# MLP layer of a two-layer kernel: part of the first activation and the add of x on GpSimd, the feature read from its PSUM bank, four more second-layer blocks on VectorE

## The reference

```python
f = lrelu(conv1x1(gn(x), sw1, sb1))      # 128 -> 64
f = lrelu(conv1x1(f, sw2, sb2))          # 64 -> 32
f = conv1x1(f, sw3, sb3)                 # 32 -> 16
# feat: the 16 features of each pixel, joined with one of 128 depth points in -1..1
h = lrelu(conv1x1(feat, mw1, mb1))       # 17 -> 32, for each point
h = lrelu(conv1x1(h, mw2, mb2))          # 32 -> 32
h = lrelu(conv1x1(h, mw3, mb3))          # 32 -> 16
x = x + sigmoid(conv1x1(h, mw4, mb4))    # 16 -> 1, the points are the channels
```

## Time and profile before

| | us |
|---|---|
| median of 3 runs | 9821.51 (9809.74 to 9825.37) |
| profiled execution | 9827.07 |
| its span, first to last instruction | 9825.2 |

### The profile page before, as it was taken

One profiled execution on the slowest core, in us unless ns is written; L12 is line 12 of the kernel. 1 busy time (PEld: TensorE's weight loads), 2 busy tenths in 40 slices (PEclk: granted clock), 3 DMA queues, 4 the chain that ended last, 5 costly groups with the idle time before them and its releaser, 6 DMA issues. The chain is left out here.

```text
span 9825.2 us, 453859 instructions
## 1 busy us (share of the span) xinstructions
PE 9314.5 (95%) x201050; PEld 3949.9 (40%) x201050; DVE 8993.4 (92%) x10311; ACT 8370.6 (85%) x14741; POOL 5791.9 (59%) x2564
## 2 busy tenths in 40 slices
PE   7999998999899999899989999989998999998999
PEld 4555553222455555222245555522224555552222
DVE  6999998999699999899979999989997999998998
ACT  5888887999778888799978788879997887887999
POOL 5999993000699999300069999930007999992000
PEclk9999998999999999899999999999999999999999
DMA  3333331000233333100023333310002333321000
GB/s 102 81 82 88 83 84 44 31 31 27 66 81 87 84 81 86 40 31 31 27 69 87 81 81 84 84 43 29 30 27 73 87 81 82 87 80 32 21 22 18
DMA packets 377226, 605.60 MB, mean 62 GB/s; under 512 B 96962, under 2 KB 98148, under 8 KB 374756
## 3 DMA queue, kind: packets, MB, share of 16 engines
q1 hardware_dynamic: 370752, 574.99, 21.0%
q10 hardware_dynamic: 4516, 1.57, 0.1%
HBM read 236.45 MB, written 71.30 MB: 31 GB/s over the span
## 5 line engine op out<-in xcount | busy, mean ns | idle before, releaser
L927 DVE TENSOR_TENSOR_SCAN arena<-arena,carried,ps 128x512 f32<-128x512 f32 x3968 | 4754.3, 1261 | 294.2 <-PE ps L446 287.9
L815 POOL TENSOR_TENSOR arena<-arena 128x1024 f32<-128x1024 f32 x2048 | 4798.2, 2382 | 148.1 <-PE ps L457 53.2
L975 DVE SCALAR_TENSOR_TENSOR arena<-arena,neg_p 128x512 f32<-128x512 f32 x4096 | 2762.8, 747 | 0.4
L699 ACT ACTIVATE arena<-arena,a_neg 128x512 f32<-128x512 f32 x4096 | 2662.8, 710 | 35.6 <-DVE arena L927 30.8
L446 PE MATMUL ps<-arena 64*32 64x128 f32 x131072 | 2335.8, 275 | 107.9 <-DVE arena L927 57.5
L754 ACT ACTIVATE arena<-ps,b2t 128x512 f32<-128x512 f32 x3840 | 2334.8, 699 | 70.3 <-PE ps L540 44.3
L446 PEld LDWEIGHTS ps<-arena 64*32 64x32 f32 x131072 | 1849.8, 106 | 1234.4 <-DVE arena L927 696.5
L823 POOL TENSOR_TENSOR arena<-arena 128x1024 f32<-128x1024 f32 x128 | 307.6, 2403 | 2969.7 <-DVE arena L919 2968.2
L540 PE MATMUL ps<-arena,w2s 32*32 32x512 f32 x32768 | 1578.5, 603 | 53.6 <-ACT arena L754 35.5
L761 ACT ACTIVATE arena<-ps,bm 128x1024 f32<-128x1024 f32 x1024 | 1165.3, 1138 | 6.1 <-PE ps L551 6.1
L551 PE MATMUL ps<-arena,m 64*32 64x512 f32 x16384 | 1120.7, 599 | 8.6 <-ACT arena L761 4.9
(11 more groups left out here) (111 smaller groups left out, 6570.0 us busy)
## 6 DMA issues: line engine op xcount, KB each, us to landing
arena<-arena SPq DMA_DIRECT2D x4096, 64.0 KB, 2.0
arena<-c_d SPq DMA_DIRECT2D x1024, 128.0 KB, 2.9
xr<-in_x SPq DMA_DIRECT2D x128, 256.0 KB, 3.2
x_d<-xr SPq DMA_DIRECT2D x128, 256.0 KB, 3.3
xr<-x_d SPq DMA_DIRECT2D x128, 256.0 KB, 3.0
out<-arena SPq DMA_DIRECT2D x128, 256.0 KB, 2.0
xs<-in_x SPq DMA_DIRECT2D x96, 256.0 KB, 3.2
arena<-in_x SPq DMA_DIRECT2D x4, 2048.0 KB, 14.9
```

Source lines behind the costliest of these rows:

```text
L699: A(dA[(UNITS * t + m) % DR][:, gi, :], drep[:, e, :], ACT.Exp, scale=a_neg[:, e, 2 * gp + gi:2 * gp + gi + 1]).then_inc(s_dA, 1)
L815: nc.gpsimd.tensor_tensor(hc[m % CR], H[:, m % HR, :, :], crep[:, 2 * gp:2 * gp + 2, :], ALU.mult).then_inc(s_ch, 1)
L927: V.tensor_tensor_scan(H[:, m % HR, gi, :], dA[(UNITS * t + m) % DR][:, gi, :], dbu[m % 2].rearrange("p (l g) -> p g l", g=2)[:, gi, :], 0 ...
L975: m = V.scalar_tensor_tensor(out=t1[k % 4][:, q, :], in0=g[par], scalar=neg_p[:, i:i + 1], in1=gs_[par], op0=ALU.max, op1=ALU.add)
```

## The change

1. SHARED goes from (1, 3) to (0, 1, 2, 3, 4, 6): VectorE does bank 3 of leaky2 in six groups, ScalarE 26 blocks per chunk instead of 30. VectorE's two instructions are rewritten: the first makes 0.01 (m2 + bias) in one pass, the second takes the maximum of (m2 + bias), read from PSUM again, and that. mm2's second half waits for the second one (s_hv) instead of the first (s_hb).
2. BY_POOL: of leaky1's four blocks Pool does block 3 in even groups and blocks 2 and 3 in odd groups, 12 of 32 per chunk. It uses a tensor_scalar (max) for each block, from `g`, and one tensor_tensor (add of `gs_`, repeated over the blocks) for each group. mm2 waits for s_lp too.
3. VectorE's leaky1 reads the feature from `f_ps` in PSUM for all groups (LATE = 8). The bank must hold until the chunk's last leaky1, so the feature's first two products go to bank 6 (`m4_ps`), between one chunk's sigmoid and the next one's first mm4, and the third product waits for s_l1 of all eight groups.
4. The order moves: the feature products go to k = 2, 3 and 5, mm4 to k = 4, 5, 7 (and 1), `spread_g` to k = 6, and leaky2(k) comes before leaky1(k+2) on VectorE.
5. The sdf add goes to Pool, behind its leaky1(4), and for the last chunk of a batch element behind its leaky1(7).

```diff
-SHARED = (1, 3)
+SHARED = (0, 1, 2, 3, 4, 6)
+BY_POOL = ((3,), (2, 3))
+R1, AHEAD, LATE = 4, 2, 8
@@ features, tensor engine
-                    pe.wait_ge(s_g, t)
-                    mm(f_ps[0:64], s1r[:, :], xr[place], start=True, stop=True).then_inc(s_f1, 1)
+                    pe.wait_ge(s_sg, t - 1 if i else t)
+                    mm(m4_ps[0:64], s1r[:, :], xr[place], start=True, stop=True).then_inc(s_f1, 1)
...
-                    mm(f_ps[0:32], s2[:, :], f1, start=True, stop=True).then_inc(s_f2, 1)
+                    mm(m4_ps[0:32], s2[:, :], f1, start=True, stop=True).then_inc(s_f2, 1)
...
                     pe.wait_ge(s_f2l, t + 1)
+                    pe.wait_ge(s_l1, (t - 1) * NG + LATE)
                     mm(f_ps, gw[:, :], f2, start=True, stop=True).then_inc(s_gp, 1)
@@ mm2
                 pe.wait_ge(s_l1, t * NG + (k + 1))
+                pe.wait_ge(s_lp, t * NG + (k + 1))
...
-                        pe.wait_ge(s_hb, t * len(SHARED) + SHARED.index(k - 1) + 1)
+                        pe.wait_ge(s_hv, t * len(SHARED) + SHARED.index(k - 1) + 1)
@@ mm4
                     pe.wait_ge(s_sg, t)
+                    pe.wait_ge(s_f2l, t + 2 if ahead else t + 1)
@@ layer1, tensor engine
-                    if k in (3, 5, 7):
-                        mm4(t, (k - 3) // 2)
                     if k == 1 and not first:
-                        mm4(t - 1, NG // 2 - 1)
-                    if ahead:
-                        if k == 0:
-                            f_a()
-                        if k == 2:
-                            f_b()
-                        if k == 4:
-                            f_c()
+                        mm4(t - 1, NG // 2 - 1, True)
+                    if ahead and k == 2:
+                        f_a()
+                    if ahead and k == 3:
+                        f_b()
+                    if k == 4:
+                        mm4(t, 0, ahead)
+                    if k == 5:
+                        mm4(t, 1, ahead)
+                    if k == 7:
+                        mm4(t, 2, ahead)
+                    if ahead and k == 5:
+                        f_c()
@@ gpsimd, new
+            def leaky1(t, k, par):
+                n = t * NG + k + 1
+                qs = BY_POOL[k % len(BY_POOL)]
+                q0, w = qs[0], len(qs)
+                pool.wait_ge(s_g, t + 1)
+                pool.wait_ge(s_m2, t * (2 * NG) + 2 * (k - R1 + 1))
+                for q in qs:
+                    i = GQ * k + q
+                    m = nc.gpsimd.tensor_scalar(t1[k % R1][:, q, :], g[par], neg_p[:, i:i + 1], None, ALU.max)
+                m.then_inc(s_lm, 1)
+                pool.wait_ge(s_lm, n)
+                v = t1[k % R1][:, q0:q0 + w, :]
+                add = gs_[par].rearrange("p (o l) -> p o l", o=1).to_broadcast([P, w, L])
+                nc.gpsimd.tensor_tensor(v, v, add, ALU.add).then_inc(s_lp, 1)
...
+            def layer1(b, i):
+                t, par = b * T + i + 1, i % 2
+                for k in range(NG):
+                    leaky1(t, k, par)
+                    if k == 4 and i > 0:
+                        sdf(t - 1, b, i - 1)
@@ vector
+                qs = BY_POOL[k % len(BY_POOL)]
                 for q in range(GQ):
-                    i = GQ * k + q
-                    m = V.scalar_tensor_tensor(out=t1[k % 4][:, q, :], in0=g[par], scalar=neg_p[:, i:i + 1], in1=gs_[par],
-                                               op0=ALU.max, op1=ALU.add)
+                    if q not in qs:
+                        i = GQ * k + q
+                        m = V.scalar_tensor_tensor(out=t1[k % R1][:, q, :], in0=f_ps if k < LATE else g[par], scalar=neg_p[:, i:i + 1], in1=gs_[par],
+                                                   op0=ALU.max, op1=ALU.add)
...
-                V.tensor_scalar(v, m2_ps[:, 3, :], b2t[:, GQ * k + 3:GQ * k + 4], None, ALU.add).then_inc(s_hb, 1)
+                V.tensor_scalar(v, m2_ps[:, 3, :], bias, SLOPE, ALU.add, ALU.mult).then_inc(s_hb, 1)
                 dve.wait_ge(s_hb, n)
-                V.scalar_tensor_tensor(out=v, in0=v, scalar=SLOPE, in1=v, op0=ALU.mult, op1=ALU.max).then_inc(s_hv, 1)
+                V.scalar_tensor_tensor(out=v, in0=m2_ps[:, 3, :], scalar=bias, in1=v, op0=ALU.add, op1=ALU.max).then_inc(s_hv, 1)
...
-                    if k == 5 and ahead:
+                    if k == 6 and ahead:
                         spread_g(t + 1, 1 - par)
-                    if k + 2 < NG:
-                        leaky1(t, k + 2, par)
-                    elif ahead:
-                        leaky1(t + 1, k + 2 - NG, 1 - par)
                     if k in SHARED:
                         leaky2(t, k)
-                    if k == 5 and not first:
-                        sdf(t - 1, b, i - 1)
+                    if k + AHEAD < NG:
+                        leaky1(t, k + AHEAD, par)
+                    elif ahead:
+                        leaky1(t + 1, k + AHEAD - NG, 1 - par)
```

More of the change, by code:

```diff
@@ L195, in mamba_sdf_kernel @@
                       s_t2: 2 * NG, s_t3: NG, s_sg: 1}
-        pool_counts = {s_du: 1, s_dg: 2, s_ch: UNITS}
+        pool_counts = {s_du: 1, s_dg: 2, s_ch: UNITS, s_lm: NG, s_lp: NG, s_ob: 1}
         dve_counts = {s_xn: 1, s_del: 1, s_scan: 2 * UNITS, s_sk: 2, s_yg: 2, s_res: 1, s_st1: 1,
-                      s_g: 1, s_l1: NG, s_hb: len(SHARED), s_hv: len(SHARED), s_ob: 1}
+                      s_g: 1, s_l1: NG, s_hb: len(SHARED), s_hv: len(SHARED)}
         def chunk_zero(eng, counts):
@@ L540, in mm2 @@
                             m = mm(m2_ps[32 * q:32 * q + 32, j, :], w2s[32 * j:32 * j + 32, :],
-                                   t1[k % 4][32 * j:32 * j + 32, q, :], start=True, stop=True)
+                                   t1[k % R1][32 * j:32 * j + 32, q, :], start=True, stop=True)
                     m.then_inc(s_m2, 1)
@@ L553, in mm3, with mm4 @@
                 m.then_inc(s_m3, 1)
-            def mm4(t, v):
+            def mm4(t, v, ahead):
                 pe.wait_ge(s_t3, t * NG + (2 * v + 2))
@@ L599, in _ @@
                 mm3(t9, NG - 1)
-                mm4(t9, NG // 2 - 1)
+                mm4(t9, NG // 2 - 1, False)
         @block.scalar
@@ L738, in first_layer @@
                     act.wait_ge(s_f2, t)
-                    A(f1, f_ps[0:64], ACT.Prelu, bias=b1r[:, :], alpha=SLOPE).then_inc(s_f1l, 1)
+                    A(f1, m4_ps[0:64], ACT.Prelu, bias=b1r[:, :], alpha=SLOPE).then_inc(s_f1l, 1)
                 def second_layer():
@@ L743, in second_layer @@
                     act.wait_ge(s_gp, t)
-                    A(f2, f_ps[0:32], ACT.Prelu, bias=bs2[:, :], alpha=SLOPE).then_inc(s_f2l, 1)
+                    A(f2, m4_ps[0:32], ACT.Prelu, bias=bs2[:, :], alpha=SLOPE).then_inc(s_f2l, 1)
                 return first_layer, second_layer
@@ L848, in layer0, with sdf @@
                         diagonals(t + 1, 1, 0)
+            def leaky1(t, k, par):
[12 more added lines that the diff above has]
+                nc.gpsimd.tensor_tensor(v, v, add, ALU.add).then_inc(s_lp, 1)
+            def sdf(t, b, i):
+                place, loaded = ring(b, 1, i)
+                pool.wait_ge(s_x[place], loaded)
+                pool.wait_ge(s_sg, t + 1)
+                pool.wait_ge(s_out[i % 2], 16 * (b * PAIRS + i // 2 + 1))
+                nc.gpsimd.tensor_tensor(ob[i % 2], sg, xr[place], ALU.add).then_inc(s_ob, 1)
+            def layer1(b, i):
[4 more added lines that the diff above has]
+                        sdf(t - 1, b, i - 1)
             for b in range(B):
@@ L852, in _ @@
                     layer0(b, i)
+                for i in range(T):
+                    layer1(b, i)
+                sdf(b * T + T, b, T - 1)
         @block.vector
@@ L982, in leaky2 @@
                 dve.wait_ge(s_m3, t * NG + (k - 3))
[L983 to L984 removed]
+                v, bias = t2[k % 4][:, 3, :], b2t[:, GQ * k + 3:GQ * k + 4]
+                V.tensor_scalar(v, m2_ps[:, 3, :], bias, SLOPE, ALU.add, ALU.mult).then_inc(s_hb, 1)
                 dve.wait_ge(s_hb, n)
[L986 to L993 removed]
+                V.scalar_tensor_tensor(out=v, in0=m2_ps[:, 3, :], scalar=bias, in1=v, op0=ALU.add, op1=ALU.max).then_inc(s_hv, 1)
             def layer1(b, i):
[L996 removed]
+                t, par, ahead = b * T + i + 1, i % 2, real(i + 1)
                 for k in range(NG):
[L998 removed]
+                    if k == 6 and ahead:
                         spread_g(t + 1, 1 - par)
[L1000 to L1003 removed]
                     if k in SHARED:
                         leaky2(t, k)
[L1006 to L1007 removed]
+                    if k + AHEAD < NG:
+                        leaky1(t, k + AHEAD, par)
+                    elif ahead:
+                        leaky1(t + 1, k + AHEAD - NG, 1 - par)
                     if k == 7 and b + 1 < B:
@@ L1034, in _ @@
                 spread_g(t1st, 0)
-                for k in range(2):
+                for k in range(AHEAD):
                     leaky1(t1st, k, 0)
```

6 lines of the change are left out of this document (3 added, 3 removed).

## The result

| | before | after |
|---|---|---|
| median | 9815.74 us (4 runs) | 10752.05 us (4 runs) |
| profiled execution | 9827.07 us | 10744.28 us |
| ratio | | 1.0949, 95% interval 1.0935 to 1.0963 |

The forecast was 9687 us, between 9545 and 9870, faster with a chance of 0.79. The time lies outside, on the other side.

What follows compares the result with a forecast made beforehand. The prediction took VectorE with its feature wait to bound the MLP stages, ScalarE close behind. A chunk falling from 27.45 to 26.4 us saves 1.05 on 4 x 32 chunks, 134 us: 9827.1 to 9693, median 9687, range 9545 to 9870.

Steps and rivals of the forecast that it cites:

- What bounds the kernel now: MLP stage, 27.45 us a chunk: VectorE with feature wait 27.5, ScalarE 26.8, TensorE 25.3; relief must reach both VectorE and ScalarE.
- ScalarE: ScalarE's activations per chunk: 4 blocks fewer at 0.57 us, so 26.8 falls to 24.5 us.
- VectorE: VectorE's sum per chunk: 20 first activations, six leaky2 pairs at 1.46; 23.8 us, with the feature wait 25.0.
- Rival 4: VectorE's PSUM reads are slower by 0.1 us, 27.0 us a chunk with the feature wait, 9764 us; chance 0.05.
- Pool: Pool's new work per chunk: 12 tensor_scalar at 0.75 us, adds, sdf and waits; sum 25.0 us, hidden within 26.4.
- 12p + 16.0: Pool's sum per chunk in us, with p the unknown time of one tensor_scalar, taken as 0.75.
- upper bound, 1.17: Pool's tensor_scalar takes at most 1.17 us, half of its two-input, two-block product L815 at 2.33.
- Rival 2: Pool sets the MLP stage, slower: 9784 us at p = 0.93, 10153 at 1.17; chance 0.18.
- Range and chances: Whole kernel: 9545 to 9870 us; faster 0.79, same 0.06, slower 0.15; about 0.11 above the range.
- p = 0.95: Time in us of Pool's tensor_scalar above which Pool's sum passes 27.45 us a chunk; chance 0.13.
- Contention: VectorE beside Pool: one SBUF input runs free; two would exclude Pool, at least 38.2 us a chunk, 11203 in all.
- TensorE's walk: One chunk walked through TensorE's matmuls: mm2's second half late about 1.1 us in all, so 26.4 us instead of 25.3.

Runs made afterwards that it cites:

- e10: The kernel before the change, with only the sdf add (x added to the sigmoid) moved from VectorE to Pool: 9823.48 us, ratio 0.9999.
- e2: The changed kernel with Pool's 12 tensor_scalar per chunk left out, so that Pool only adds: 9649.84 us, ratio 0.9829.
- e1: A kernel without both layers, timing Pool's and VectorE's instruction forms alone and side by side; Pool's tensor_scalar took 1.54 us alone.
- e3: The changed kernel with LATE = 0, so VectorE's leaky1 reads the feature from g in SBUF: 11217.09 us, ratio 1.1421.
- e5: The changed kernel with Pool taking 8 blocks instead of 12 and VectorE's second blocks at k = 0, 2, 4, 6: 9813.98 us, ratio 0.9984.

## Why the prediction was wrong, by its own steps

- **What bounds the kernel now.** The prediction had VectorE with its feature wait last and ScalarE 0.6 us behind. e10 speaks against this order: VectorE took 0.4 us more per chunk there at no cost. ScalarE's 26.8 was too low as well; it was busy 694.6 us for 25.5 chunks, 27.2 each. By exclusion ScalarE and TensorE, which wait for each other through mm2's banks, set the 27.45; no run relieved ScalarE alone. In e2 both ScalarE and VectorE were relieved and Pool was cheap: 26.3.
- **ScalarE.** 26 blocks per chunk at 0.57, right (521 L763 in 20 chunks).
- **VectorE.** Right within 0.02 in each term: L1017 742 ns (0.73 to 0.75), the leaky2 pair 750 and 751 ns (0.75 and 0.73). Rival 4, slower PSUM reads, is out.
- **Pool.** This is the step that failed: "I take 0.75, nearer the lower end, since L832 shows that Pool's cost follows what it reads". The op takes 1.54 to 1.56, so 12p + 16.0 gives 34.5 to 34.7 where 25.0 stood. It also lies above the upper bound, 1.17. That bound assumed that one input can't cost more than two, and no row said so: it compared different ops. The one-block adds were 0.08 low, 1.25 from start to start. With 34.9 for 26.4 the prediction's own formula gives 27.45 + 7.45 = 34.9 a chunk, 10775 us, 0.2% from the result.
- **Range and chances.** Rival 2 had the mechanism, a chance of 0.18 and a top of 10153. The range closed at 9870 by weighing values between two bounds that were none. With the only Pool form unknown, 12 times per chunk, and a threshold at p = 0.95, close to L832's halved row at 0.93, the chance of slower should have been near a half.
- **Contention.** The rule was right about which form slows down (e1, e3), and the prediction used it rightly. Its price, 38.2 us "at least", counted all of both engines' time as exclusive: that would add 13.2 us to Pool's sum, and 3.6 were measured on the chunk, with 10.7 on VectorE, mostly where it would have been idle.
- **TensorE's walk.** 26.4 against 26.3 in e2, with the releaser mistaken and a delay of 0.8 us where 0.49 was walked, made up by shorter mm2 groups: right in part by luck. The same kind of walk failed for e5 (26.6 against 27.6), where ScalarE's waits were left out.
- **The Trainium skill's rule** (GPSIMD Engine Reference, Engine selection) that one-input work runs roughly at line rate holds for the copy, 0.56 us for 512 elements where VectorE's feature copies take 0.60, and not for tensor_scalar, 1.54. Its 769 ns for a best loop (section on elementwise accounting) was no guide either.

## What to carry to other kernels

An operation that no row of the trace shows is unbounded above until it has been timed; a dearer-looking operation of the same engine is no ceiling. When work moves to an idle engine, write its sum with the unknown as a letter, find the value at which it turns the sign, and let the chance of a loss be the chance of that value. On four engines within 10% of each other, compare circles (who waits for whom around one chunk) and not sums alone.

## What the runs showed of the hardware

- Pool, 128x512 fp32, per instruction in a row: copy 0.56, product with a repeated column 1.00, add 1.22, tensor_scalar max 1.45 with an immediate and 1.54 with a pointer. Two adds in one instruction 2.30 (e1, L116, 36.79 / 16).
- A VectorE instruction with two SBUF inputs and a Pool instruction that reads SBUF lengthen each other; with one of the inputs in PSUM neither does. Beside Pool's add the two run nearly one after the other (37.4 us for the pair, 40.8 in turn), beside its tensor_scalar they mostly overlap (28.4, 45.8 in turn). Even one Pool add per chunk took more from VectorE, 0.9 us, than the 0.6 it gave (e10).
- The granted clock of TensorE was 0.89 in the stretch of the changed kernel and 1.00 before. The levels are seen in the timeline above: the weight loads at 2009.13 came 0.84 us after the ones before them, those at 2006.43 and 2008.14 after 1.67 and 1.48, about twice as long. The granted clock was 0.54 from 2004.30 to 2006.40, 0.56 from there to 2008.10 and 1.00 from there on, 1.2 and 2.4 GHz in the main; the weight loads had stood idle for 2.8 us ahead of the slow stretch. It cost nothing that shows here: Pool's instructions follow each other without a gap, so Pool set the chunk. e2 had 1.00 again.
